# An attention and sparse feed-forward block on one core: five score banks in attention's last three units, and batch 0's marks made one tile ahead instead of two in its first four rounds

## What is computed

```python
x = layernorm(x + attention(x, wq, wk, wv, wo))   # 32 heads of 16, 8 key/value heads
inter = xf @ c1_w.T @ c2_w.T                      # rank 16, 1792 columns, 56 blocks of 32
idx = argmax(inter in each block) + block start   # one column of each block per token
h = relu(w1[idx] . xf)
x = layernorm(x + sum(h * w2t[idx]))
```

## Time and profile before

| | |
|---|---|
| Median of 3 executions | 831.04 us (830.64 and 1455.67 the ends) |
| The profiled execution | 832.09 us, span 830.3 us, mean granted clock of TensorE 0.992 |
| PE busy | 801.7 us (97%) |
| VectorE (DVE) busy | 642.8 us (77%) |
| ScalarE (ACT) busy | 387.0 us (47%) |
| GpSimd (POOL) busy | 336.5 us (41%) |
| Chain that ended last | PE 86%, DVE 5%, ACT 4%, issue 2%, DMA 2% |

### The profile page before, as it was taken

One profiled execution on the slowest core, in us unless ns is written; L12 is line 12 of the kernel. 1 busy time (PEld: TensorE's weight loads), 2 busy tenths in 40 slices (PEclk: granted clock), 3 DMA queues, 4 the chain that ended last, 5 costly groups with the idle time before them and its releaser, 6 DMA issues.

```text
span 830.3 us, 11435 instructions
## 1 busy us (share of the span) xinstructions
PE 801.7 (97%) x4040; PEld 499.5 (60%) x4040; DVE 642.8 (77%) x827; ACT 387.0 (47%) x712; POOL 336.5 (41%) x444
## 2 busy tenths in 40 slices
PE   6999999999999999999999989999999999999994
PEld 5866433343333333333337768878878888788883
DVE  5588899999999999999216887878867887688763
ACT  4321688888888888888761321231311031112111
POOL 2212243753575455323411653433433343334441
PEclk9999999999999999999999989999999999999998
DMA  7684263344554454333406721240400030002001
GB/s 227 237 275 140 73 159 84 107 111 118 157 145 110 124 159 125 90 102 109 117 14 223 249 73 33 64 140 2 139 14 1 1 111 16 1 1 73 29 1 51
DMA packets 48192, 83.09 MB, mean 100 GB/s; under 512 B 9528, under 2 KB 13624, under 8 KB 48008
## 3 DMA queue, kind: packets, MB, share of 16 engines
q1 hardware_dynamic: 40448, 64.45, 25.5%
q0 software_dynamic: 7408, 16.81, 6.8%
q10 hardware_dynamic: 280, 1.11, 0.5%
HBM read 54.23 MB, written 28.05 MB: 99 GB/s over the span
## 4 chain that ended last, share of the span: by engine, by line
PE 86%; DVE 5%; ACT 4%; issue 2%; DMA 2%; SPq 0%; POOL 0%; ACTq 0%; POOLq 0%; DVEq 0%
PE ps_h L1246 18%; PE ps_pair L1263 18%; PE ps_pv L660 15%; PE ps_st L646 14%; PE ps_pair L633 6%; PE ps_st L608 6%; ACT probs L492 2%; PE ps_pv L608 2%; PE ps_pair L673 2%; ACT stage L463 1%; PE ps_prep L1223 1%; PE ps_prep L1218 1%; DVE neg_max L526 1%; PE ps_prep L1210 1%; DMA yf<-x 1%
## 5 line engine op out<-in xcount | busy, mean ns | idle before, releaser
L526 DVE TENSOR_REDUCE neg_max<-ps_pair 128x2 f32<-128x1024 f32 x256 | 301.4, 1219 | 30.6 <-PE ps_pair L633 30.6
L492 ACT ACTIVATE probs<-ps_st 128x512 f32<-128x512 f32 x512 | 266.3, 606 | 58.7 <-PE ps_st L646 57.7
L646 PE MATMUL ps_st<-q,k 50*128 50x512 f32 x512 | 185.1, 448 | 2.5 <-ACT probs L492 0.4
L646 PEld LDWEIGHTS ps_st<-q,k 50*128 50x128 f32 x512 | 83.3, 185 | 164.7 <-ACT probs L492 158.8
L982 ACT ACTIVATE g_h<-picked 128x512 fp32r<-128x512 f32 x56 | 35.5, 633 | 250.5 <-DVE picked L1100 250.5
L633 PE MATMUL ps_pair<-k,q 48*128 48x512 f32 x512 | 149.1, 440 | 1.8 <-DVE neg_max L526 1.8
L660 PE MATMUL ps_pv<-probs,v 128*32 128x512 f32 x1024 | 136.4, 605 | 0.0
L899 POOL TENSOR_TENSOR g_l<-picked,g_h 128x512 fp32r<-128x512 f32 x56 | 72.5, 1294 | 127.6 <-ACT g_h L982 127.6
L1246 PE MATMUL ps_h<-xt_h,w_h 128*128 128x512 f32 x224 | 90.6, 405 | 3.4 <-DVE picked L1100 3.4
L1246 PE MATMUL ps_h<-xt_h,w_l 128*128 128x512 f32 x224 | 89.8, 401 | 0.0
L1246 PE MATMUL ps_h<-xt_l,w_h 128*128 128x512 f32 x224 | 89.6, 400 | 0.0
(11 more groups left out here) (152 smaller groups left out, 1141.8 us busy)
## 6 DMA issues: line engine op xcount, KB each, us to landing
operands<-parts POOLq DMA_DIRECT2D x20, 512.0 KB, 3.6
q<-operands SPq DMA_DIRECT2D x64, 128.0 KB, 2.7
sums<-stage SPq DMA_DIRECT2D x32, 256.0 KB, 3.1
x_raw<-xT SPq DMA_DIRECT2D x16, 256.0 KB, 5.1
k<-operands SPq DMA_DIRECT2D x64, 64.0 KB, 2.3
q<-operands SPq DMA_DIRECT2D x64, 64.0 KB, 2.5
att<-sums SPq DMA_DIRECT2D x16, 256.0 KB
yf<-x SPq DMA_DIRECT2D x4, 1024.0 KB, 7.1
```

What stands on the lines that cost most here:

```text
L492: nc.scalar.activation(probs[kt % 2][:, r], ps_st[i % 3][:], ACT.Exp, scale=float(HD) ** -0.5).then_inc(exp_done, 1)
L526: nc.vector.tensor_reduce(neg_max[:, at:at + 2], ps_max[pair % 2][:], AX.X, ALU.max, negate=True).then_inc(max_red, 1)
L646: nc.tensor.matmul(ps_st[i % 3][:], k_[n % QR][64 * a:64 * a + ROWS, kt * P:(kt + 1) * P], q[n % QR][64 * a:64 * a + ROWS, j, :], start=Tr ...
```

## The change

Attention. From tile WIDE = (32 - 3) x 16 on, that is in the last three units, the transposed scores go round five banks: the three of `ps_st` and the two of `ps_max[1]`. The first two tiles in `ps_max[1]` wait for the last row maximum (`max_red`), and the later ones for the exponential of the tile five before. s3 moves in front of `weigh`. The output projection has only the two banks of `ps_max[0]`, so that row tile t >= 2 waits for the addition of t-2.

Feed-forward, batch 0. VectorE's mark step is cut in two: `step` keeps the transpose, and `first_in_block` has the rest. The order of VectorE becomes: ..., pick 0, addition (2,2), marks 1, addition (2,3), turn 1, pick 1, two statistics; rounds 1 to 3: pick i (from 2 on), marks i+1, turn i+1; round 4: transpose 5, late addition, pick 4, rest of marks 5, turn 5, marks 6; and from round 5 on as before. The other engines' orders there are not changed.

```diff
@@ -90,6 +90,7 @@
     LOADS = 8
     PRE = 2 * REP + 5
     FIRST_MAXIMA = 2 * TASKS - 1
+    WIDE = (NU - AHEAD) * TILES
     with ExitStack() as ctx:
         sb = lambda name, shape, dt=F32: ctx.enter_context(nc.sbuf_tensor(name, shape, dt))
         sem = lambda name: ctx.enter_context(nc.semaphore(name))
@@ -140,6 +141,13 @@
 
         def bank(i):
             return (*ps_st, ps_pv)[i % 4]
+
+        def score_bank(i):
+
+            if i < WIDE:
+                return ps_st[i % 3]
+            return (ps_st[WIDE % 3], ps_st[(WIDE + 1) % 3], ps_max[1][:, 0], ps_max[1][:, 1], ps_st[(WIDE + 2) % 3]
+                    )[(i - WIDE) % 5]
 
         def part(b, o):
 
@@ -489,7 +497,7 @@
                         act.wait_ge(st_mm, i + 1)
                         if r == 0 and n * TT + kt >= 2:
                             act.wait_ge(pv_done, n * TT + kt - 1)
-                        nc.scalar.activation(probs[kt % 2][:, r], ps_st[i % 3][:], ACT.Exp,
+                        nc.scalar.activation(probs[kt % 2][:, r], score_bank(i)[:], ACT.Exp,
                                              scale=float(HD) ** -0.5).then_inc(exp_done, 1)
             take_sums(NU - 1)
 
@@ -541,7 +549,7 @@
 
             def add_residual(t):
                 dve.wait_ge(wo_done, t + 1)
-                nc.vector.tensor_tensor(y0[:, t], ps_max[t // 2][:, t % 2], y0[:, t], ALU.add).then_inc(added, 1)
+                nc.vector.tensor_tensor(y0[:, t], ps_max[0][:, t % 2], y0[:, t], ALU.add).then_inc(added, 1)
                 dve.wait_ge(added, t + 1)
                 nc.vector.bn_stats(stats[:, t], y0[:, t]).then_inc(stat_done, 1)
 
@@ -640,10 +648,14 @@
                     pe.wait_ge(shift_in[n % QR], 2 * DMA * (n // QR + 1))
                 if i < 3:
                     task_taken(pe, max(j for j in range(LAST) if j % 4 == i))
+                elif i < WIDE + 2:
+                    pe.wait_ge(exp_done, i - 2)
+                elif i < WIDE + 4:
+                    pe.wait_ge(max_red, NT // 2)
                 else:
-                    pe.wait_ge(exp_done, i - 2)
+                    pe.wait_ge(exp_done, i - 4)
                 a, j = r % 2, r // 2
-                nc.tensor.matmul(ps_st[i % 3][:], k_[n % QR][64 * a:64 * a + ROWS, kt * P:(kt + 1) * P],
+                nc.tensor.matmul(score_bank(i)[:], k_[n % QR][64 * a:64 * a + ROWS, kt * P:(kt + 1) * P],
                                  q[n % QR][64 * a:64 * a + ROWS, j, :], start=True, stop=True).then_inc(st_mm, 1)
 
             def weigh(n, kt):
@@ -668,9 +680,11 @@
                     pe.wait_ge(max_red, NT // 2)
                     pe.wait_ge(pre, PRE)
                     pe.wait_ge(att_split, REP)
+                if t >= 2 and third == 0:
+                    pe.wait_ge(added, t - 1)
                 for i in range(4 * third, 4 * third + 4):
                     r, (a, w) = i // 3, ((att_h, wo_h), (att_h, wo_l), (att_l, wo_h))[i % 3]
-                    last = nc.tensor.matmul(ps_max[t // 2][:, t % 2], a[0][:, r, t * P:(t + 1) * P], w[:, r],
+                    last = nc.tensor.matmul(ps_max[0][:, t % 2], a[0][:, r, t * P:(t + 1) * P], w[:, r],
                                             start=(i == 0), stop=(i == 11))
                 if third == 2:
                     last.then_inc(wo_done, 1)
@@ -695,9 +709,12 @@
                     scores(ahead)
                     scores(ahead + 1)
                     scores_t(n, kt, 2)
+                    if n >= NU - AHEAD:
+                        scores_t(n, kt, 3)
                     if step:
                         weigh(*divmod(step - 1, TT))
-                    scores_t(n, kt, 3)
+                    if n < NU - AHEAD:
+                        scores_t(n, kt, 3)
                     scores(ahead + 2)
                     scores(ahead + 3)
                     if n >= NU - AHEAD:
@@ -1061,27 +1078,31 @@
                     if i:
                         dve.wait_ge(reached_ready, i)
                     nc.vector.transpose(ps_turned[:].rearrange("p n k -> p (n k)"), bank[:]).then_inc(prep_done, 1)
-                    dve.wait_ge(prep_done, n + 1)
...
+
+            def first_in_block(i):
+
+                b, m = divmod(i, MT)
+                dve.wait_ge(prep_done, number(b, marks(m)) + 1)
+                if i == 0:
+                    dve.wait_ge(constants, 4)
+                nc.vector.tensor_tensor_scan(
+                    ps_turned[:].rearrange("p n k -> p (n k)"), gate[:].rearrange("p n k -> p (n k)"),
+                    ps_turned[:].rearrange("p n k -> p (n k)"), 0.0, ALU.min, ALU.max).then_inc(scanned, 1)
+                dve.wait_ge(scanned, i + 1)
+                nc.vector.tensor_copy(top[:], ps_turned[:, :, BLK - 1]).then_inc(topped, 1)
+                dve.wait_ge(topped, i + 1)
+                if i:
+                    dve.wait_ge(marks_ready, i)
+                nc.vector.tensor_tensor(
+                    reached[:, :, 1:], ps_turned[:],
+                    top[:].rearrange("p (n o) -> p n o", o=1).broadcast_to([P, S // BLK, BLK]),
+                    ALU.is_equal).then_inc(reached_ready, 1)
+                if i < MT:
+                    dve.wait_ge(reached_ready, i + 1)
                     if i:
+                        dve.wait_ge(mask_t_ready, i)
+                    nc.vector.tensor_tensor(marked[:], reached[:, :, 1:], reached[:, :, :BLK], ALU.subtract
+                                            ).then_inc(marks_ready, 1)
 
             def turn_marks(i):
 
@@ -1149,27 +1170,36 @@
             add_residual(2, 1)
             front(U)
             front(marks(0))
+            first_in_block(0)
             turn_marks(0)
             pick(0, 0)
             add_rows(2, 2)
             front(marks(1))
+            first_in_block(1)
+            add_rows(2, 3)
             turn_marks(1)
             pick(0, 1)
-            add_rows(2, 3)
             row_statistics(2, 2)
             row_statistics(2, 3)
             for b in range(NB):
                 for m in range(MT):
                     i, steps = b * MT + m, slot_steps(b, m)
+                    if i == 4:
+                        step(0, marks(i + 1))
                     for following in steps:
                         if not U < following[1] <= marks(MT - 1):
                             step(*following)
                     if i >= 2:
                         pick(b, m)
+                    if 1 <= i <= 3:
+                        step(0, marks(i + 1))
+                    if 1 <= i <= 4:
+                        first_in_block(i + 1)
                     if 2 <= i + 1 < NB * MT:
                         turn_marks(i + 1)
-                    if i + 2 < NB * MT:
+                    if 4 <= i < NB * MT - 2:
                         step(*steps[-1])
+                        first_in_block(i + 2)
                     if b and m == 0:
                         add(b - 1)
                     if b and m == 1:
```

More of the change, by code:

```diff
@@ L1070, in step @@
-                    dve.wait_ge(scanned, i + 1)
-                    nc.vector.tensor_copy(top[:], ps_turned[:, :, BLK - 1]).then_inc(topped, 1)
-                    dve.wait_ge(topped, i + 1)
-                    if i:
[L1074 to L1084, removed]
+            def first_in_block(i):
[17 more added lines that the diff above has]
+                    dve.wait_ge(reached_ready, i + 1)
+                    if i:
+                        dve.wait_ge(mask_t_ready, i)
+                    nc.vector.tensor_tensor(marked[:], reached[:, :, 1:], reached[:, :, :BLK], ALU.subtract
+                                            ).then_inc(marks_ready, 1)
```

## The result

The changed kernel takes 820.52 us (median of 4, 820.09 to 821.56); the kernel before took 830.84 beside it (median of 4; one of these took 1455.67 and is left out of the ratio). The ratio of the means is 0.9888, with a 95% interval of 0.9862 to 0.9915: 1.1% faster. The forecast was 821.8, the range 819.5 to 827.0.

The account below looks back on a forecast made before the run. The PE was taken to bound the kernel. Gains of 4.4 (attention) + 5.5 (rounds) - 0.1 = 9.8 us gave 822.3 from the profiled 832.09 and 821.2 from the median; forecast 821.8, range 819.5 to 827.

Parts of the forecast that it names:

- Terms 1 and 2: Attention's last twelve steps: s3 free beside s2 makes steps 2.78 us; the first loses 0.34; net 4.4 us gained.
- rival B: Attention's last three units: s3 not free beside s2, 0.15 gained a step instead of 0.43; 824.9 us; chance 0.12.
- Term 3: Attention's output projection: with two banks, row tile t waits for the addition of t-2; costs nothing.
- Term 4: Batch 0's first rounds: addition (2,3) ahead of the mask turn lets up(2) start 0.78 us earlier.
- Term 5: Pick 2 before tile 3's marks: up(3) 3.09 us earlier, a 1.1 us pause remains, no clock fall saves 3.08 again.
- Term 6: Batch 0's round 3: two VectorE collisions with POOL counted; up(4) waits and 0.69 us is given back.
- Terms 4 to 6: Batch 0's first rounds up to up(4), summed: 5.5 us gained, 6.2 without collisions.
- Term 7: Batch 0's rounds 4 to 6: one tile less of lead is made up here; 0.1 us lost.
- rival C: Rounds 4 to 6: VectorE stays behind through collisions in three subtractions; 2 us lost, 823.8 us; chance 0.06.
- rival A: Batch 0's rounds: the clock still falls once, priced 3.08 less 0.69 us; 824.2 us; chance 0.17.
- Rival D: Attention's first step and before up(3), up(4), up(6): clock falls after each short pause; slower, 834.1 us; chance 0.03.

Follow-up runs that it names:

- e1: Attention's half of the change alone, batch 0's rounds as in the kernel before: 826.65 us, ratio 0.9949.
- e11: Kernel before with pick 2 ahead of tile 3's marks, but addition (2,3) left behind pick 1: 826.17 us, ratio 0.9943.
- e12: Kernel before with only the addition (2,3) moved ahead of turn 1 and pick 1: 829.85 us, ratio 0.9985.
- e3: Kernel before with five score banks and two projection banks, s3 still behind the weighting: 831.79 us, ratio 1.0016.
- e4: Kernel before with s3 ahead of the weighting, but three score banks and four projection banks: 835.96 us, ratio 1.0063.
- e9: Changed kernel with one statistic moved from ahead of marks 2 to behind pick 2: 821.72 us, ratio 0.9889 against the kernel before.
- e2: The rounds' half of the change alone, attention as in the kernel before: 824.86 us, ratio 0.9928.
- e7: Changed kernel with six extra 512-column statistics on VectorE ahead of pick 2: 825.38 us, ratio 0.9929 against the kernel before.
- e6: Changed kernel with three extra 512-column statistics on VectorE ahead of pick 2: 822.26 us, ratio 0.9895 against the kernel before.
- e8: Changed kernel with s2 and s3 behind the weighting in the first of the twelve steps only: 819.97 us, ratio 0.9869 against the kernel before.

## Why the prediction was right, and where it was not

- **Terms 1 and 2** (4.4 us): 4.19 in the trace, 4.25 in e1's median. s3 is free beside s2 (rival B falls by the 0.66 for four), the step 2.785 for 2.78. The first step's loss was 0.11 too small.
- **Term 3** (nothing): right. The two projection banks never made the PE wait.
- **Term 4**: up(2) starts 36.19 us behind the seam; it was 474.48 - 437.23 = 37.25. That is 1.06, for 0.78 forecast. By e11 and e12 this head start alone is worth nothing; I had counted it in the path, and there it only made the pause before up(3) longer, as long as one remained.
- **Term 5**: the mechanism was right, the size was not. I had held that marks 2 would "keep their times". They came 0.27 us earlier (40.19 for 40.46 behind the seam). GpSimd's tile came 0.12 earlier too (40.25 for 40.37); the other 0.15 is the addition's move into a gap (0.13 in e12, where it moves alone). It turned a start 0.09 behind that tile into one 0.06 ahead. So the subtraction won, pick 2 ended 1.3 us earlier than forecast (42.16 behind the seam for 43.48), and the pause of 1.1 did not appear at all.
- **Term 6**: I counted two collisions in round 3. The first took 0.81 for an estimated 0.86; the second did not occur: the variance line took 0.17 (479.44) beside GpSimd's pair at 478.04. It takes 0.17 in every run with the new order and 0.83 to 0.86 in every one with the old. The traces tell the two apart: in the old order it begins 0.65 us into a GpSimd instruction and ends with it, in the new one it begins in the last 0.1 us of one. No edit tested this alone. The 0.69 given back was 0. Round 3 took 5.91 us by the timeline (42.21 to 48.12) for 5.80, because the first matmul behind the wait is followed after 0.34 us (474.77, 475.11) and not 0.23. Terms 4 to 6 thus gave 7.23 at up(4) for 5.5: up(3) is 1.33 earlier than forecast, and round 3, by the chain, 6.07 for 6.49.
- **Term 7** (0.1 lost): none. The rounds from up(4) on are 8.51 and 8.52 us, and later collisions (489.31, 1.48 us) are hidden, so rival C falls.
- **The clock**: I priced the fall at 3.08 by an undisturbed round of 5.80 (the 8.88 beside it ends at a start of the chain, 8.72 is the like of 5.80). Without a fall the old order's round took 6.58 in e3 and 6.60 in e12, since VectorE held up(4) back by 0.5 as well. By up(6), counted from up(3), these two took 23.90 and 23.92 us, the profiled execution before 25.91, e1 and e4 24.62 and 24.61: the fall cost 2.0 in the first and 0.7 in the others. So rival A was priced too high, and the profiled execution before was a dear one, by 1.3 us over e1's and e4's. That accounts for most of the difference between the traces' gain of 11.9 and the medians' 10.3. Against the profiled execution my 9.8 was short by the collisions that did not come and by the 0.48 of scatter; against the medians that was nearly made up by a fall which, as far as e1 and e4 show, the median execution has less of. That the sum came out better than its terms is luck.
- **Rival D** (several falls) needed falls behind pauses of about 1 us. None followed pauses of 1.05, 1.06, 1.09 or 1.43.

## What to carry to other kernels

When an engine works two tiles ahead, look at what stands in front of the operation that the bottleneck waits for; one tile less of lead can cost nothing, as long as the lead is not used up at a later join. An order and its buffers are one change: here five banks alone cost 0.9 us, the order alone 5.1, and both together gain 4.2. Price a pause by executions with and without it, since what one profile shows behind it may be a draw.

## What the hardware showed that was not expected

VectorE's subtraction with both operands in SBUF takes 0.44 us beside an idle GpSimd and up to 1.64 beside its instructions. What is left of the GpSimd instruction in progress tells how long. In the kernel before:

```profile
477.60 1.28 POOL L920 TENSOR_TENSOR xt_l<-att,xt_h 128x512 fp32r<-128x512 f32 x1
...
488.24 1.46 POOL L920 TENSOR_TENSOR xt_l<-att,xt_h 128x512 fp32r<-128x512 f32 x1
```

Marks 2's subtraction begins at 477.69, when 1.19 us of the first are left, and takes 1.05 more than 0.44. The variance line begins at 488.90, when 0.80 of the second are left, and takes 0.66 more than 0.17. In e9 0.69 left cost 0.55; in the changed kernel's marks 3 0.51 left cost 0.37. The fourteen traces have 63 such cases with 0.16 us or more left, and in each the wait is what is left, less 0.14. Of the 15 that begin with 0.08 to 0.11 left, 14 wait for nothing.

So it turns on hundredths only when VectorE asks at the very end of an instruction. The subtraction began 0.06 (changed), 0.04 (e2, e12), 0.06 (e7) and 0.07 us (e6) ahead of GpSimd's next instruction and took 0.44, but 0.05 ahead in e8 it took 1.64, having waited for the whole of that next one. Begun 0.09 to 0.12 behind a start, it always took 1.46 to 1.50. "SBUF — State Buffer" in the Trainium skill, "Who interferes with whom", has the first to issue hold the port for its whole instruction; five of the six agree, and e8 does not by the recorded starts. In e12 one addition's move brought the start 0.13 us forward against GpSimd's tile, and the end 1.2.

The half-speed clock (1.2 of 2.4 GHz) followed a pause of 3.40 to 3.42 us in three profiled executions and not a pause of 3.39 in a fourth, nor of 3.17 or 2.96. Where it came it lasted differently long: from 483.5 to 490 the windows of the kernel before are at 0.50, in e1 from 480 to 483. In the kernel before it fell while the PE still stood idle: the granted clock is 1.00 to 483.0 and 0.75 from there to 483.5, and up(3) starts at 483.86.
